# A DLRM tower on one core: the units split 114/81 in the first block and 82/113 in the later ones (from 110/85), the layer 1 matrix reloaded once, and a newly planned order

## The chip, the core and the metric

The kernel runs on one core of a Trainium2 chip, in float32. The metric is the device time of one execution in microseconds. The profile is one execution, recorded on that core; its page gives the span from the first to the last instruction, and this span is what the rows below are about.

## What is computed

```python
e = jnp.stack([tbl_0[ids[:, 0]], ..., tbl_39[ids[:, 39]]], axis=1)   # 2048 x 40 x 64
i_idx, j_idx = np.triu_indices(40, k=1)                             # 780 pairs
viW = jnp.einsum('bpd,pde->bpe', e[:, i_idx, :], W)                 # W: 780 x 64 x 64
z = jnp.einsum('bpe,bpe->bp', viW, e[:, j_idx, :])
h = jnp.concatenate([z, dense_ctx], axis=1)                         # 2048 x 796
h = jnp.maximum(h @ W_top1 + b_top1, 0.0)                           # 796 x 512
h = jnp.maximum(h @ W_top2 + b_top2, 0.0)                           # 512 x 256
y = h @ W_top3                                                      # 256 x 1
```

Each of 2048 examples looks up 40 rows of 64 numbers. For each of the 780 pairs of fields, one row goes through a 64x64 matrix and is multiplied with the other row and summed over 64. The 780 sums and 16 dense inputs go through three layers.

## The kernel before, in words

The batch is worked in four blocks of 512 examples. Two neighbouring fields form a duo, so there are 20 duos, and four duos form a quad, so there are 5 quads. A block has 190 pairings of two different duos (four field pairs each) and 20 pairs inside the duos. Its work on TensorE is cut into 195 **units**, and each unit ends in one product of 128x1024 numbers on VectorE (DVE).

- A standing unit (F, line 1007) holds weights still and streams the transposed rows `x`. Its result lies with the 64 numbers of a pair along the partitions, so VectorE writes the product to `fprod` (line 1172) and TensorE has to sum it with a matmul against `ones` into `z_ps` (line 1032). One unit has two such sum tiles; four tiles go side by side in one **round**, so two F units take one round.
- A moving unit (R, line 1003) holds `x` still and streams weights. Its result has the 64 numbers along the row, so no TensorE sum is needed. The product (line 1163, line 1158 for the inner units I) is summed over 64 by one of three engines: ScalarE (ACT, tile `rprod_A`, 16 activations with an accumulator each, line 1234), VectorE (`rprod_V`, one reduce, line 1180) or GpSimd (POOL, `rprod_P`, six additions, lines 919 and 926). The sums are gathered in `zb`, which TensorE turns later in pieces (event `zr`, line 1049).

`MOVED` says for each quad how many of the duos go by R units. Before, it is `[0, 3, 4, 5, 8]` for all blocks: 110 F units, 80 R units (four per pairing of a quad with a duo) and 5 I units in each block.

Around the units TensorE turns looked-up rows into `x` (event `duo`, line 965; the first four duos come from tables on chip instead, line 958), and runs the three layers of the block before (events `l1`, `l2`, `l3`; four `l1` of 7 passes each, line 1063, two `l2`, line 1073). The first-layer matrix `w1_sb` lies in `mlp_sb`, loaded once by SP at line 874. Its rows stand in the order in which the sums come out, so that order depends on the split of the units.

Three semaphore rings couple the engines. `u_ps` has `U_SLOTS` = 3 places: unit u waits until the product of unit u-3 is done. `fprod` has 9 places, freed by the TensorE sums. `rprod` has 3, 2 and 2 places for A, V and P, freed by the sum over 64. Weights come in by SP through `wf_ring` (4 places of two F units, line 829) and `wr_ring` (2 places of four R units, line 835).

The order on every engine is fixed when the program is built. The class `Plan` walks through the work with a small clock of its own: it has a duration for each kind of step, picks the next step for TensorE (unit, sum, duo or layer step), gives each R unit's sum to A, P or V, and places GpSimd's lookups (line 899) between its sums. Before, sums go in groups of `GROUP` = 4 F units, which are two rounds. Lookups of later blocks carry waits on `mains_done`, so that on average over six of them they start no closer than `T_PACE` = 1.6 us:

```python
if len(self.gather_at) >= PACE_OVER:
    gather_at = max(gather_at, self.gather_at[-PACE_OVER] + PACE_OVER * T_PACE)
```

In the first block, each lookup is followed by a memset of a spare piece (line 908) that keeps them apart.

Of the kernel before, what the change touches and what calls it, by code (L numbers as in the profile page):

```python
# [35 lines left out]
P = 128  # L36
# [10 lines left out]
MOVED = [0, 3, 4, 5, 8]  # L47
FOLD = 2 * 8
GROUP = 4
HALF = GROUP // 2  # L50
# [6 lines left out]
Z_SPARE = 2  # L57
# [20 lines left out]

STANDING = [("F", n, k) for n in range(DUOS) for k in range(MOVED[n // 4], n)]
CHUNKS_R = [(q, k) for q in range(QUADS) for k in range(MOVED[q])]  # L80
MOVING = [unit for q in range(QUADS) for unit in
          [("R", c, s) for c, (of, _) in enumerate(CHUNKS_R) if of == q for s in range(SUBS)] + [("I", q, 0)]]
NF, NR = len(STANDING), len(MOVING)
NC = len(CHUNKS_R)
GROUPS = -(-NF // GROUP)

HALVES = NF // HALF
NT = 2 * NF
Z_TILES = 64
K_GROUPS = Z_TILES // (2 * GROUP)  # L90
ZF = -(-NT // Z_TILES)
Z_LAST = NT - Z_TILES * (ZF - 1)
R_PAIRS = NC * FOLD + DUOS
ZR = -(-R_PAIRS // P)
ZK = ZF + ZR

ZB_SLOTS = ZR + 2
DENSE = 16

STRIPS = 4  # L100

DENSE_CHUNK, DENSE_ROW = ZK - 1, R_PAIRS % P
assert 0 < DENSE_ROW <= P - DENSE


def z_rows(k):

    if k == DENSE_CHUNK:
        return DENSE_ROW + DENSE
    return P if k < ZF else min(P, R_PAIRS - P * (k - ZF))  # L110


W1_COLS, W2_COLS = ZK * H1, M1 * H2
assert NF % HALF == 0 and Z_TILES % (2 * GROUP) == 0

# [11 lines left out]
def tile_pairs(f, half):  # L127

    _, n, k = STANDING[f]
    i, j = 2 * (DUOS - 1 - n) + half, 2 * (DUOS - 1 - k)  # L130
    return (i, j), (i, j + 1)


def moving_pair(c, half, e):

    q, k = CHUNKS_R[c]
    return 2 * (DUOS - 1 - 4 * q - e // 2) + e % 2, 2 * (DUOS - 1 - k) + half


# [4 lines left out]
def quad_of(kind, n):  # L144

    return n if kind == "I" else CHUNKS_R[n][0]


def stands(kind, n):

    return list(range(4 * n, 4 * n + 4)) if kind == "I" else [CHUNKS_R[n][1]]


def first_column(kind, n):

    return FOLD * NC + 4 * n if kind == "I" else FOLD * n


def units_until(c):

    return 1 + max(r for r, (kind, n, _) in enumerate(MOVING) if first_column(kind, n) < P * (c + 1))

def lay_standing(w):
    out = np.zeros((NF // HALF, P, HALF, P), np.float32)
    for f in range(NF):
        for half in range(2):  # L170
            for par, pair in enumerate(tile_pairs(f, half)):
                out[f // HALF, half * DIM:(half + 1) * DIM, f % HALF,
                    par * DIM:(par + 1) * DIM] = w[pair_index(*pair)]
    return out.reshape(NF // HALF, P, HALF * P)


def lay_moving(w):
    out = np.zeros((NC, P, 8, DIM), np.float32)
    for c in range(NC):
        for half in range(2):  # L180
            for e in range(8):
                out[c, half * DIM:(half + 1) * DIM, e] = w[pair_index(*moving_pair(c, half, e))].T
    return out.reshape(NC, P, 8 * DIM)
# [13 lines left out]
def lay_mlp(w1, b1, w2, b2, w3):  # L197
    lay1 = np.zeros((P, ZK, H1), np.float32)
    for t in range(NT):
        k, strip, r = z_place(t)  # L200
        for par, pair in enumerate(tile_pairs(t // 2, t % 2)):
            lay1[32 * strip + r + par, k] = w1[pair_index(*pair)]
    for c in range(NC):
        for a in range(FOLD):
            row = FOLD * c + a
            lay1[row % P, ZF + row // P] = w1[pair_index(*moving_pair(c, a // 8, a % 8))]
    for n in range(DUOS):
        row = first_column("I", n // 4) + n % 4
        lay1[row % P, ZF + row // P] = w1[pair_index(*inner_pair(n))]
    n_pairs = FIELDS * (FIELDS - 1) // 2  # L210
    lay1[DENSE_ROW:DENSE_ROW + DENSE, DENSE_CHUNK] = w1[n_pairs:]
    lay2 = w2.reshape(M1, P, H2).transpose(1, 0, 2)
    return np.concatenate([lay1.reshape(P, -1), lay2.reshape(P, -1), b1.reshape(M1, P).T, b2.reshape(M2, P).T,
                           w3.reshape(M2, P).T], axis=1)

T_UNIT, T_SUMS, T_DUO, T_PASS, T_TURN = 0.846, 0.41 * GROUP, 0.44, 0.858, 0.17
T_PROD, T_VSUM, T_PART, T_COPY, T_RELU = 1.131, 1.127, 0.48, 0.58, 0.69
# [5 lines left out]
T_INNER = 1.75  # L230
T_HOT, T_BUILD, T_TABLE, T_TABLES = 0.423, 0.535, 8.5, 1.6

LEAD, LEAST, ROWS_LEAD = 8, 1, 5

STALL, GAP = 0.05, -0.3

MLP_GAP, MLP_PACE = 8, 14

AHEAD, BEHIND = 2, 10
# [3 lines left out]
A_MOST, P_MOST = 1, 1  # L243


def tail_of(b):

    return [("l1", b, m) for m in range(M1)] + [("l2", b, m) for m in range(M2)] + [("l3", b, 0)]


class Plan:


    def __init__(self):
# [8 lines left out]
        self.queue = {e: [] for e in "VAP"}  # L263
        self.parts = []
        self.gathered, self.built = 2 * SUBS * HOT, 0
        self.gather_at, self.main_at, self.paced = [], [], 0
        self.need = 0
        self.f_units, self.r_units = [], []
        self.rows_of = {}
# [1051 lines left out]
```

## Time and profile before

| what | value |
|---|---|
| time, three runs | 1356.27 us median (1356.18 to 1361.23) |
| profiled execution, span | 1195.2 us |
| profiled execution, own time | not given apart from the span; median less span is 161.1 us, outside the first to last instruction |
| granted TensorE clock | 1.000 over the whole span |
| TensorE busy | 1177.7 us, 99% |
| VectorE busy | 1003.0 us, 84% |
| ScalarE busy | 966.7 us, 81% |
| GpSimd busy | 774.4 us, 65% |
| DMA | 79.7 MB, mean 67 GB/s |

Matmuls are recorded one by one though they overlap, so the busy share says that TensorE seldom stands still, and the chain of waits says what it does in that time. TensorE's first unit starts at 37.5 us; the first units of blocks 2, 3 and 4 start at 307.1, 592.0 and 875.4 us, and the last unit ends near 1155 us.

### The profile page before, as it was taken

What the parts mean: (1) busy time and instruction counts of PE and PEld (TensorE: products, weight loads), DVE (VectorE), ACT (ScalarE), POOL (GpSimd) and SP (SyncE); (2) the same over time, 40 slices, a digit from 0 to 9 for tenths busy, and PEclk for the clock granted to TensorE, in tenths of its full rate; (3) what the DMA queues carried; (4) which work ended last, traced back from release to release, by engine and by line L of the source; (5) the groups of instructions that cost most, each with busy time, mean ns of one, the idle gap of its engine ahead of it and who ended that gap; (6) DMA issues with size and microseconds to landing.
All of it is one profiled execution on the core that took longest, in us unless ns stands there. A gap on an engine that the chain in (4) does not pass through costs nothing.

```text
span 1195.2 us, 23954 instructions
## 1 busy us (share of the span) xinstructions
PE 1177.7 (99%) x6248; PEld 457.7 (38%) x6248; DVE 1003.0 (84%) x915; ACT 966.7 (81%) x7477; POOL 774.4 (65%) x1026
## 2 busy tenths in 40 slices
PE   7999999999999999999999999999999999999999
PEld 2433333333434343333434343433343434343333
DVE  7898999999588888999877878889978778888960
ACT  1295989899476799999687879999969899999971
POOL 8888883687656556677755557887765556634320
PEclk9999999999999999999999999999999999999999
DMA  7143232222222222222222222222222222211100
GB/s 211 38 148 78 65 75 65 70 72 72 57 56 68 56 67 73 68 67 70 71 55 63 60 64 65 71 63 78 73 57 59 59 66 63 66 45 55 49 10 0
DMA packets 68480, 79.73 MB, mean 67 GB/s; under 512 B 15308, under 2 KB 46028, under 8 KB 68216
## 3 DMA queue, kind: packets, MB, share of 16 engines
q1 hardware_dynamic: 48752, 58.10, 16.6%
q0 software_dynamic: 19456, 19.96, 9.3%
q8 instruction: 50, 0.82, 0.3%
q14 instruction: 86, 0.70, 0.2%
q10 hardware_dynamic: 136, 0.14, 0.1%
HBM read 78.14 MB, written 0.01 MB: 65 GB/s over the span
## 4 chain that ended last, share of the span: by engine, by line
PE 89%; DVE 5%; issue 4%; ACT 1%; POOL 1%; DMA 0%; SPq 0%; DVEq 0%; ACTq 0%; POOLq 0%
PE u_ps L1007 30%; PE u_ps L1003 23%; PE z_ps L1032 16%; PE turn_ps L1063 7%; PE turn_ps L965 3%; PE u_ps L997 3%; PE turn_ps L958 2%; DVE fprod L1172 2%; PE turn_ps L1073 2%; PE u_ps L1063 2%; DVE acts L1128 1%; DVE zb L1180 1%; DVE rprod_A L1163 1%; PE u_ps L1073 1%; ACT rprod_A L1234 1%
## 5 line engine op out<-in xcount | busy, mean ns | idle before, releaser
L1234 ACT ACTIVATE rprod_A<-rprod_A 128x64 f32<-128x64 f32 x3664 | 877.8, 243 | 95.2 <-DVE rprod_A L1163 66.5
L899 POOL DMA_INDIRECT rows<-in_tbl,ids_all x608 | 575.2, 946 | 288.6 <-issue 113.5
L1234 ACT ACTIVATION_READ_ACCUMULATOR rprod_A<-rprod_A 128x1 f32 x3664 | 691.6, 189 | 0.1
L1172 DVE TENSOR_TENSOR fprod<-u_ps,x 128x1024 f32<-128x1024 f32 x440 | 524.0, 1222 | 32.1 <-PE u_ps L1007 31.9
L1007 PE MATMUL u_ps<-x,wf_ring 64*128 64x512 f32 x1760 | 444.9, 604 | 2.3 <-DVE fprod L1172 0.7
L1163 DVE TENSOR_TENSOR rprod_A<-u_ps,rows 128x1024 f32<-128x1024 f32 x213 | 260.5, 1224 | 98.0 <-PE u_ps L1003 97.8
L1003 PE MATMUL u_ps<-wr_ring,x 64*128 64x512 f32 x1280 | 338.7, 614 | 0.1
L1007 PEld LDWEIGHTS u_ps<-x,wf_ring 64*128 64x128 f32 x1760 | 158.6, 186 | 219.4 <-issue 163.9
L1032 PE MATMUL z_ps<-fprod,ones 128*32 128x512 f32 x1760 | 212.4, 598 | 0.0
L919 POOL TENSOR_TENSOR rprod_P<-rprod_P 128x512 f32<-128x512 f32 (+4 forms) x235 | 142.5, 606 | 81.7 <-DVE rprod_P L1163 58.6
L1003 PEld LDWEIGHTS u_ps<-wr_ring,x 64*128 64x128 f32 x1280 | 110.2, 185 | 172.7 <-issue 92.8
L1032 PEld LDWEIGHTS z_ps<-fprod,ones 128*32 128x32 f32 x1760 | 45.9, 109 | 147.1 <-issue 73.2
L1217 ACT COPY x<-turn_ps 128x512 f32<-128x512 f32 x80 | 45.5, 569 | 55.1 <-PE turn_ps L958 29.9
L1063 PE MATMUL turn_ps<-acts,mlp_sb 128*128 128x512 f32 (+1 forms) x182 | 81.6, 599 | 0.9 <-ACT acts L1249 0.9
L1180 DVE TENSOR_REDUCE zb<-rprod_V 128x16 f32<-128x1024 f32 x64 | 77.5, 1225 | 1.2
L1163 DVE TENSOR_TENSOR rprod_V<-u_ps,rows 128x1024 f32<-128x1024 f32 x62 | 75.4, 1226 | 0.1
L1163 DVE TENSOR_TENSOR rprod_P<-u_ps,rows 128x1024 f32<-128x1024 f32 x45 | 55.0, 1223 | 2.7 <-PE u_ps L1003 2.7
L965 PEld LDWEIGHTS turn_ps<-ident,rows 128*128 128x128 f32 x304 | 31.8, 140 | 57.0 <-issue 55.4
L1063 PEld LDWEIGHTS turn_ps<-acts,mlp_sb 128*128 128x128 f32 (+1 forms) x182 | 33.5, 190 | 47.6 <-issue 46.5
L965 PE MATMUL turn_ps<-ident,rows 128*128 128x128 f32 x304 | 49.9, 286 | 0.0
L958 PE MATMUL turn_ps<-acts,mlp_sb 125*64 125x512 f32 x136 | 36.4, 622 | 9.8 <-DMA mlp_sb<-in_tbl 7.8
L908 POOL MEMSET zb<- 128x256 f32 x128 | 46.0, 360 | 0.1
(45 smaller groups left out, 299.4 us busy)
## 6 DMA issues: line engine op xcount, KB each, us to landing
wf_ring<-in_w_standing SPq DMA_DIRECT2D x220, 128.0 KB
wr_ring<-in_w_moving SPq DMA_DIRECT2D x80, 256.0 KB
rows<-in_tbl,ids_all POOLq DMA_INDIRECT x608, 2.5
mlp_sb<-in_mlp SPq DMA_DIRECT2D x1, 2308.0 KB
mlp_sb<-in_tbl SPq DMA_DIRECT2D x6, 224.0 KB
wi_ring<-in_w_inner SPq DMA_DIRECT2D x20, 64.0 KB, 1.8
rows<-in_first_ids SPq DMA_DIRECT2D x4, 256.0 KB, 6.2
rprod_P<-in_first_ids SPq DMA_DIRECT2D x4, 256.0 KB, 8.8
```

What stands on the lines that cost most here:

```text
L899: nc.gpsimd.indirect_dma_start(rows[:, v % ROW_SLOTS, s, par * DIM:(par + 1) * DIM], None, tables[f], bass.IndirectOffsetOnAxis(ap=ids_all ...
L919: nc.gpsimd.tensor_tensor(of[:, :, 0:width], of[:, :, 0:width], of[:, :, width:2 * width], ALU.add).then_inc(fold_step, 1)
L958: op = pe.matmul(bank[h % 2 * DIM:(h % 2 + 1) * DIM, :], tables_sb[:, at:at + DIM], hot[0:HOT_PARTS, i % HOT_SLOTS, :], start=(c == 0), st ...
L965: op = pe.transpose(bank[:, s * P:(s + 1) * P], rows[:, v % ROW_SLOTS, s, :], ident[:])
L1003: op = pe.matmul(u_ps[:, bank + half, :], x[on, x_slot(b, of[0]), k * P:(k + 1) * P], wr_ring[on, c % WR_SLOTS, :], start=True, stop=True)
L1007: op = pe.matmul(u_ps[:, bank + half, :], wf_ring[on, c % WF_SLOTS, f % HALF * P:(f % HALF + 1) * P], x[on, x_slot(b, n), :], start=True, ...
L1032: op = pe.matmul(z_ps[32 * strip:32 * strip + 32, :], ones[:, 30 - row:62 - row], fprod[:, f % FPROD_SLOTS, t % 2, :], start=(r < STRIPS), ...
L1063: op = pe.matmul(bank[:, :], w1_sb[0:n_rows, k, m * P:(m + 1) * P], z_sb[0:n_rows, z_slot(b, k), :], start=(k == 0), stop=(k == ZK - 1))
L1163: nc.vector.tensor_tensor(products_of(u).rearrange("p h (a d) -> p h a d", a=4), u_ps[:, bank:bank + 2, :].rearrange("p h (a d) -> p h a d ...
L1172: nc.vector.tensor_tensor(fprod[:, f % FPROD_SLOTS], u_ps[:, bank:bank + 2, :], other, ALU.mult).then_inc(prods_done, 1)
L1180: nc.vector.tensor_reduce(to, of.rearrange("p (a s) d -> p a s d", a=to.shape[1]), AX.X, ALU.add).then_inc(r_sums["V"], 1)
L1234: op = nc.scalar.activation(of[:, j, :], of[:, j, :], ACT.Copy, accum_out=sum_at(u, j))
```

## The change

Each block has its own shape: `MOVED` becomes a list of four splits. The first block has 114 F, 76 R and 5 I units, each later one 82 F, 108 R and 5 I. The first-layer matrix is laid out for both splits, and SP loads the second layout once, after the first block's last `l1`. Sums are taken by rounds (one to three at once) instead of by groups of two rounds. The planner has new durations and rules; `T_PACE` becomes 1.25, the duration it has for one lookup, for all blocks but the first. Inner sums, `zb` and the ring of `z` tiles get new places. The number of 128-row pieces that layer 1 reads stays at 7.

```diff
-MOVED = [0, 3, 4, 5, 8]
+MOVED = [(0, 4, 4, 4, 7), (0, 4, 4, 7, 12), (0, 4, 4, 7, 12), (0, 4, 4, 7, 12)]
...
-GROUP = 4
-HALF = GROUP // 2
+HALF = 2
...
-T_GATHER, T_ROWS, T_FOLD = 1.25, 2.5, 3.3
-T_PACE, PACE_OVER, AHEAD_OF = 1.6, 6, 1.0
+T_GATHER, T_ROWS, T_FOLD = 1.25, 2.5, 3.65
+T_PACE, T_PACE_FIRST, PACE_OVER, AHEAD_OF = 1.25, 1.6, 6, 1.0
...
-AHEAD, BEHIND = 2, 10
+AHEAD, BEHIND = 0, 4
...
-A_MOST, P_MOST = 1, 1
+SUM_LEAST, SUM_MOST, SUM_WAIT, FOLLOW = 1, 3, 0.2, 0
+CHAIN = 0
+A_MOST, P_MOST, V_MOST = 2, 2, 1
...
+    def sums_ready(self, at):
+        if self.next_half() is None:
+            return 0
+        b, h = self.next_half()
+        n, stop = 0, min(SHAPES[b].halves, (h // Z_HALVES + 1) * Z_HALVES)
+        while h + n < stop:
+            ready = self.half_ready(b, h + n)
+            if ready is None or ready > at:
+                break
+            n, at = n + 1, at + T_ROUND
+        return n
...
+W1_AFTER = {unit_after(("l1", b, M1 - 1)): b for b in range(NB - 1) if KIND_OF[b] != KIND_OF[b + 1]}
...
-                    sp.dma_start(mlp_sb[:], mlp_w).then_inc(mlp_in, 16)
+                    sp.dma_start(mlp_sb[:], mlp_w[KIND_OF[0]]).then_inc(mlp_in, 16)
+                if u in W1_AFTER:
+                    old = W1_AFTER[u]
+                    sp.wait_ge(turned, TURN_AT["l1", old, M1 - 1] + 1)
+                    sp.dma_start(mlp_sb[:, 0:W1_COLS], mlp_w[KIND_OF[old + 1]][:, 0:W1_COLS]).then_inc(mlp_in, 16)
```

Over the program, as counted in the two orders: F units 440 before and 360 now, R units 320 and 400, sum rounds 220 and 180, sum batches 112 and 126, `zr` turns 12 and 15, duos 80 and 80, layer steps the same. The sums over 64 of R and I units lie on ACT, V and P as 229, 64 and 47 before, and as 251, 103 and 66 now. By block, V has 25, 20, 13 and 6 before and 18, 33, 35 and 17 now; P has 7, 10, 13 and 17 before and 2, 16, 15 and 33 now; ACT has 53, 55, 59 and 62 before and 61, 64, 63 and 63 now.

TensorE's order in the second block, before; `z_ps<-fprod,ones` is a batch of sums (x8 is two rounds), `u_ps<-x,wf_ring` an F unit for each x2, `u_ps<-wr_ring,x` an R unit for each x2, `turn_ps<-ident,rows` a duo:

```order
L1003 MATMUL u_ps<-wr_ring,x 128x512 x2
L1007 MATMUL u_ps<-x,wf_ring 128x512 x2
L1003 MATMUL u_ps<-wr_ring,x 128x512 x2
L1007 MATMUL u_ps<-x,wf_ring 128x512 x2
L1032 MATMUL z_ps<-fprod,ones 32x512 x8
L1003 MATMUL u_ps<-wr_ring,x 128x512 x2
L1007 MATMUL u_ps<-x,wf_ring 128x512 x2
```

The same engine in the second block now; `turn_ps<-acts,mlp_sb` x7 is one `l1`:

```order
L1111 MATMUL z_ps<-fprod,ones 32x512 x4
L1085 MATMUL u_ps<-x,wf_ring 128x512 x2
L1081 MATMUL u_ps<-wr_ring,x 128x512 x2
L1111 MATMUL z_ps<-fprod,ones 32x512 x4
L1081 MATMUL u_ps<-wr_ring,x 128x512 x2
L1085 MATMUL u_ps<-x,wf_ring 128x512 x2
L1043 MATMUL turn_ps<-ident,rows 128x128 x4
L1081 MATMUL u_ps<-wr_ring,x 128x512 x2
L1143 MATMUL turn_ps<-acts,mlp_sb 128x512 x7
L1081 MATMUL u_ps<-wr_ring,x 128x512 x8
L1111 MATMUL z_ps<-fprod,ones 32x512 x4
```

A batch is often one round where it was always two (one at the end of a block), R units follow one another, and fewer F units stand between the batches.

GpSimd's order where the first block's lookups end, before; each `in_tbl` row is a run of lookups, each `rprod_P` row a step of one sum over 64:

```order
L908 MEMSET zb 128x256
L899 DMA rows<-in_tbl_38,ids_all 128x64 x4
L899 DMA rows<-in_tbl_39,ids_all 128x64 x4
L899 DMA rows<-in_tbl_36,ids_all 128x64 x4
L899 DMA rows<-in_tbl_37,ids_all 128x64 x2
L919 TENSOR_TENSOR rprod_P<-rprod_P 128x16x32
```

GpSimd at the same place now:

```order
L986 MEMSET zb 128x256
L977 DMA rows<-in_tbl_38,ids_all 128x64 x4
L977 DMA rows<-in_tbl_39,ids_all 128x64 x4
L977 DMA rows<-in_tbl_36,ids_all 128x64 x4
L977 DMA rows<-in_tbl_37,ids_all 128x64 x4
L977 DMA rows<-in_tbl_34,ids_all 128x64 x4
```

There were 14 lookups before the first sum over 64; now 64 stand in a row before it. Of the lookups and sums together, 344 lookups carried a wait on `mains_done` before, and 336 do now, in other places.

SP's order at the new load, now (`mlp_sb<-in_mlp` 128x3584 is the second layout of the first-layer matrix); before, the row is not there:

```order
L900 DMA wf_ring<-in_w_standing 128x256
L907 DMA wr_ring<-in_w_moving 128x512
L900 DMA wf_ring<-in_w_standing 128x256
L952 DMA mlp_sb<-in_mlp 128x3584
L907 DMA wr_ring<-in_w_moving 128x512
L913 DMA wi_ring<-in_w_inner 128x128
L900 DMA wf_ring<-in_w_standing 128x256 x2
```

One load of 1792 KB now stands ahead of the ring loads behind it.

## Rows read from the trace of the kernel before

**Rows 1.** The page: busy time, share of the span and instructions of each engine.
```profile
PE 1177.7 (99%) x6248; PEld 457.7 (38%) x6248; DVE 1003.0 (84%) x915; ACT 966.7 (81%) x7477; POOL 774.4 (65%) x1026
```

**Rows 2.** Windows: first block, second, third, fourth, tail; PE, PEld, DVE, ACT, POOL busy.
```profile
37.50:307.10 269.60, 266.89 (x1485) 99.96 (x1484) 257.45 (x235) 222.70 (x1729) 211.09 (x310) 1.00 0.30 77
307.10:592.00 284.90, 283.89 (x1533) 111.92 (x1534) 245.09 (x215) 231.99 (x1796) 189.13 (x226) 1.00 0.27 65
592.00:875.40 283.40, 282.51 (x1530) 111.44 (x1526) 239.92 (x210) 245.13 (x1921) 197.21 (x243) 1.00 0.27 66
875.40:1154.10 278.70, 278.32 (x1493) 107.58 (x1492) 228.09 (x200) 252.27 (x1998) 145.84 (x199) 1.00 0.22 55
1154.10:1195.20 41.10, 38.00 (x110) 15.23 (x108) 3.36 (x3) 7.57 (x24) 0.00 (x0) 1.00 0.00 0
```

**Rows 3.** The chain of waits in the second block: start, length, what.
```profile
400.28 1.85 PE z_ps L1032 x16
402.13 1.06 PE u_ps L1003 x4
403.19 1.72 PE u_ps L1007 x8
404.91 0.59 PE turn_ps L965 x4
405.50 1.06 PE u_ps L1003 x4
...
408.27 6.21 PE turn_ps L1063 x14
```

**Rows 4.** The chain of waits, shares by line: stretch 150 to 306 us.
```profile
by line: PE u_ps L1007 26.9%; PE u_ps L1003 24.7%; PE z_ps L1032 13.1%; issue 12.8%; DVE fprod L1172 6.9%; DVE rprod_A L1163 3.6%; DVE zb L1180 3.0%; PE turn_ps L965 2.6%; PE u_ps L997 2.5%; ACT rprod_A L1234 1.7%; DVE rprod_V L1163 1.6%; P
```

**Rows 5.** Windows: the stretch 150 to 306 us, columns as in rows 2.
```profile
150.00:306.00 156.00, 154.50 (x854) 56.45 (x850) 154.22 (x137) 142.37 (x1130) 110.44 (x155) 1.00 0.28 70
```

**Rows 6.** Timeline of VectorE around 200 us: start, length, instruction.
```profile
200.29 1.25 DVE L1163 TENSOR_TENSOR rprod_V<-u_ps,rows 128x1024 f32<-128x1024 f32 x1
201.42 1.25 DVE L1172 TENSOR_TENSOR fprod<-u_ps,x 128x1024 f32<-128x1024 f32 x1
```

**Rows 7.** The chain of waits at a turn of `zb`, end of the second block.
```profile
590.54 0.56 PE turn_ps L1049 x4
```

**Rows 8.** Timeline of VectorE behind one `l1` of the second block; idle before in brackets.
```profile
329.18 2.36 DVE L1163 TENSOR_TENSOR rprod_A<-u_ps,rows 128x1024 f32<-128x1024 f32 x2 [7.90 <-PE u_ps L1003]
```

**Rows 9.** Groups by line: busy time, mean ns of one, idle before and its releasers.
```profile
L1234 ACT ACTIVATE rprod_A<-rprod_A 128x64 f32<-128x64 f32 x3664 | 877.8, 243 | 95.2 <-DVE rprod_A L1163 66.5 <-DVE rprod_A L1158 26.2 <-ACT acts L1269 1.3
```

**Rows 10.** Instructions that touch `mlp_sb`: the one load of the layer matrices.
```profile
L874 SPq DMA_DIRECT2D mlp_sb<-in_mlp x1: 432/432/432, 62.8 to 62.8; - x1
```

**Rows 11.** Windows: the 5 us behind that load, columns as in rows 2.
```profile
65.00:70.00 5.00, 5.00 (x28) 2.15 (x24) 4.60 (x5) 4.40 (x35) 4.39 (x8) 1.00 0.94 396
```

**Rows 12.** Timeline of GpSimd: first and last of six lookups in a row.
```profile
661.10 0.94 POOL L899 DMA_INDIRECT rows<-in_tbl,ids_all  x1 [0.30 <-issue]
...
667.35 0.94 POOL L899 DMA_INDIRECT rows<-in_tbl,ids_all  x1 [0.30 <-issue]
```

**Rows 13.** Timeline of GpSimd: one sum over 64 (without its last step), next lookup.
```profile
791.64 3.37 POOL L919 TENSOR_TENSOR rprod_P<-rprod_P 128x512 f32<-128x512 f32 x5
...
795.52 0.96 POOL L899 DMA_INDIRECT rows<-in_tbl,ids_all  x1 [0.22 <-issue]
```

**Rows 14.** Timeline of GpSimd in the first block: two lookups, a memset between.
```profile
62.84 0.95 POOL L899 DMA_INDIRECT rows<-in_tbl,ids_all  x1 [0.17 <-issue]
...
64.28 0.95 POOL L899 DMA_INDIRECT rows<-in_tbl,ids_all  x1 [0.16 <-issue]
```

**Rows 15.** Instructions of the lookups' line: min/median/max ns of all 608.
```profile
L899 POOL DMA_INDIRECT rows<-in_tbl,ids_all x608: 938/944/1097, 3.9 to 1035.0; - x152
```

**Rows 16.** The chain of waits around an inner unit, end of the second block.
```profile
583.61 1.96 PE u_ps L997 x32
...
589.41 1.13 PE u_ps L1007 x4
```

More of the change, by code:

```diff
@@ new lines, with starts @@
+KINDS = sorted(set(MOVED))
+SHAPES = [Shape(moved) for moved in MOVED]
+KIND_OF = [KINDS.index(moved) for moved in MOVED]
+ZK, ZR = max(shape.zk for shape in SHAPES), max(shape.zr for shape in SHAPES)
+Z_RING = 9 - ZR
+ZB_SLOTS = 5
+def starts(counts):
+    return [sum(counts[:b]) for b in range(NB + 1)]
+F_FROM, R_FROM = starts([shape.nf for shape in SHAPES]), starts([shape.nr for shape in SHAPES])
+HALF_FROM, Z_FROM = starts([shape.halves for shape in SHAPES]), starts([shape.zf for shape in SHAPES])
@@ L177, in lay_moving @@
-def lay_moving(w):
[L178 to L183, printed above, removed]
+def lay_standing(w):
+    out = []
+    for shape in map(Shape, KINDS):
+        part = np.zeros((shape.halves, P, HALF, P), np.float32)
+        for f in range(shape.nf):
+            for half in range(2):
+                for par, pair in enumerate(shape.tile_pairs(f, half)):
+                    part[f // HALF, half * DIM:(half + 1) * DIM, f % HALF,
+                         par * DIM:(par + 1) * DIM] = w[pair_index(*pair)]
+        out.append(part.reshape(shape.halves, P, HALF * P))
+    return np.concatenate(out)
@@ L186, in lay_inner @@
+def lay_moving(w):
+    out = []
+    for shape in map(Shape, KINDS):
+        part = np.zeros((shape.nc, P, 8, DIM), np.float32)
+        for c in range(shape.nc):
+            for half in range(2):
+                for e in range(8):
+                    part[c, half * DIM:(half + 1) * DIM, e] = w[pair_index(*shape.moving_pair(c, half, e))].T
+        out.append(part.reshape(shape.nc, P, 8 * DIM))
+    return np.concatenate(out)
 def lay_inner(w):
@@ L484, in do_back, with next_half, half_ready @@
         self.arrived[n] = self.bank_at = self.do_act(("copy", ("back", 0, n)), self.pe_t + LAG_PE, T_COPY)
-    def do_sums(self, b, g):
-        self.order.append(("sum", b, g))
-        first = NF * b + GROUP * g
+    def next_half(self):
+        h = len(self.half_at)
+        if h >= HALF_FROM[NB]:
+            return None
+        b = max(a for a in range(NB) if HALF_FROM[a] <= h)
+        return b, h - HALF_FROM[b]
+    def half_ready(self, b, h):
+        f = F_FROM[b] + HALF * h + HALF - 1
+        if f >= len(self.f_units):
+            return None
+        at = self.prod_at[self.f_units[f]]
+        return max(at, self.z_at[-1]) if h % Z_HALVES == 0 and self.z_at else at
@@ L596, in run @@
[L596 to L601 removed]
+                step_at = self.step_ready(steps[0]) if steps and turned > self.need + LEAST else None
+                soon = self.pe_t + max(stall, SOON)
@@ L1087, in _ @@
             pe.wait_ge(ones_done, 1)
-            for what, b, n in ORDER:
+            for what, b, n, *more in ORDER:
                 if what == "duo":
@@ L1095, in _ @@
                 elif what == "sum":
-                    sums(b, n)
+                    sums(b, n, more[0])
                 elif what == "zr":
```

482 lines of the change are left out of this document (254 added, 228 removed).

## The prediction

> **What bounds the kernel now.** I read the page first. TensorE is busy for 99% of the span, VectorE for 84%, ScalarE for 81%, GpSimd for 65% [rows 1]. A busy TensorE can still be a waiting one, since its records overlap, so the next view is the chain of waits. In the second block the chain is TensorE alone, one piece against the next [rows 3]: a unit takes 0.86 us, two rounds of sums 1.85, a duo 0.59, an `l1` 6.21, and the first unit behind anything that isn't a unit takes 1.06 in place of 0.86. (The trace records two instructions for each one that the order shows.) A wait there would show as a piece of another engine, and there is none.
>
> The first block is different. In the stretch 150 to 306 us the chain passes through VectorE's lines again and again, with 12.8% issue between [rows 4], and VectorE is busy 154.22 of 156 us [rows 5]. So the first block runs at VectorE's pace and the other three at TensorE's. The windows by block say the same: VectorE has 257 of 270 us in the first, 245 of 285 in the second, 240 of 283 in the third, 228 of 279 in the fourth [rows 2].
>
> **Prices.** Taken from start to start, one VectorE product or reduce is 1.13 us (200.29 to 201.42) [rows 6]. A round costs 0.86, since a batch of two rounds takes 1.85, of which 0.13 is entry. With the 0.20 that the next unit pays, each batch costs 0.33 beside its rounds [rows 3]. A duo costs 0.59 and the same 0.20, 0.79 in all; a turn of `zb` 0.56 and 0.20, 0.76 in all [rows 3, 7]. An F and an R unit cost TensorE and VectorE the same, so swapping 80 of them moves only sums.
>
> **Blocks 2 to 4, on TensorE.**
> - Each has 28 F units fewer, so 14 rounds fewer (41 for 55): 14 x 0.86 = 12.0 us, three times, -36.0.
> - Batches in this stretch grow from 86 to 87, +0.3. Although most batches are now one round, there are fewer rounds to batch.
> - Turns of `zb` grow from 9 to 14: 5 x 0.76 = +3.8.
> - Duos that stand in these blocks grow from 54 to 57 (the planner does four more in the second and one fewer in the last): 3 x 0.79 = +2.4.
> - Layer 1 keeps its 7 pieces, so the `l1` pieces of 6.21 us don't change.
>
> That is -29.5 us. By block it is -7.3 in the second, -11.2 in the third and -11.0 in the fourth.
>
> **What hides the added sums, and what it costs if the cover is thin.** VectorE gets 195 products and 33, 35 and 17 sums in the later blocks: 228, 230 and 212 instructions at 1.13, which is 258, 260 and 240 us. Without new waits the blocks would last 278, 272 and, less the tail, 268 us. So VectorE would be busy 93%, 96% and 90%, where it was at 86%, 85% and 82%. It can't use all its time: while an `l1` holds TensorE, it gets no product, and stood idle 7.90 us across one [rows 8]. Today it comes to such a step with nothing in hand. With three products in `u_ps` and two sums in `rprod_V` waiting, five instructions or 5.7 us, the hole would shrink to 2.2 us. Four `l1` then cost some 9 us a block, two `l2` little. 260 and 9 is 269, just under 272. TensorE and VectorE would be level, and level engines with a three-place ring between them lose something to each other. The lower bound is nothing. The upper is what the first block loses with VectorE saturated: 269.6 us against 220 instructions, 249 us, hence 21 us, part of which is its start. I take 2 us in each of blocks 2 and 3, near the lower end because the third block's row is still on TensorE's side: +4.
>
> ScalarE gets 251 sums for 229. A sum's 16 activations took 877.8/229 = 3.8 us busy by overlapping records [rows 9], so each later block has 63 or 64 of them, about 242 us of 270, with the copies beside them. That is up from 55 to 62. It is tight also, but a copy late by one pair of activations (0.5 us) only matters when TensorE waits for that bank; it is within the 4 us.
>
> **The first block, on VectorE.** Its V sums go from 25 to 18: 7 x 1.13 = -7.9 us where VectorE sets the pace. TensorE gets two rounds (+1.7) and 13 batches (+4.3) more there, 3 duos and 2 `zb` turns fewer (-3.9), which is +2.1; these lie in its waiting. I take -7, between -8 (all hidden) and +2 (no stall removed at all).
>
> **The reload.** SP issues 1792 KB ahead of the ring loads. The load before was 2308 KB, issued at 62.8 [rows 10]; in 65 to 70 us the DMA engines were 0.94 busy at 396 GB/s, and TensorE was busy 5.00 of 5.00 us [rows 11]. At that rate the reload takes 4.6 us. `wr_ring` holds four more R units then, at least 3.4 us of units and, with F units between, twice that. So I cost it at 0. Uncovered, it is up to 5 us, once. Nothing else waits on SP's queue but the rings, and the matrix is first read one block later.
>
> **Lookups and GpSimd.** A lookup back to back takes 1.25 us from start to start (six in a row start within 6.25 us) [rows 12], and a sum over 64 takes 3.88 until the next lookup starts [rows 13]; in the first block a lookup with its memset is 1.44 [rows 14]. At present: 47 x 3.88 + 128 x 1.44 + 480 x 1.25 = 967 us. After: 66 x 3.88 in place of 47, 1040 us, against some 1120 until the last unit ends. It still fits, with 80 us to spare, so the pacing's removal and 19 more sums cost nothing, and earlier rows remove no wait either, as the chain shows none for rows [rows 3]. The 608 lookups last 938 to 1097 ns with a median of 944 [rows 15], next to a VectorE that is nearly always at work. If more VectorE work held them back, the maximum would be far from the median already. The Trainium skill, SBUF — State Buffer, "SBUF: two separate sides", says that VectorE in a two-port mode locks GpSimd out, so that it can't write the descriptors of its transfers. [...] The trace agrees with the case in which no lock is taken.
>
> **The sum.** -29.5 + 4 - 7 = -32.5 us. The span goes from 1195.2 to 1162.7. I keep the 161.1 us around it (the median less this span; the median of three stands for the profiled one, whose own time isn't given), and get 1323.8. One more thing is in the order's favour: in the later blocks the chain still leaves TensorE now and then, as for 3.8 us behind an inner unit at 583.6 [rows 16], though TensorE has other units for a part of that. The new order is planned with durations nearer to the rows (0.858 us for a unit in place of 0.846), and may avoid some of it; I choose -2, which no row fixes. Forecast: 1322 us, 2.5% faster.
>
> **Rivals.**
> - VectorE becomes the bound in blocks 2 and 3 as it is in the first. For it: 93 and 96% by the above. Against: `l1` holes shrink when work is in hand. If these blocks lost to each other what the first loses beyond its start, about 10 us each in place of 2, the time is 1322 + 16 = 1338. From 97% of a block's length on it decides.
> - The order's gains are larger: the first block, planned with 7 fewer V sums and batches of one round, drops its waits nearly to TensorE's own work, some 12 us more. Then 1310.
> - Slower: lookups in long runs. The rows show six in a row at 1.25 [rows 12]; in the new order 64 stand in a row, with waits among them. If a lookup in a long run took what the planner spaced them at before, 1.6 us, 480 x 0.35 = 168 us would be added to GpSimd, 88 more than its spare time; rows come late, duos wait, and the time is 1322 + 88 = 1410. It decides from 1.25 + (80 + 34 + 7)/480 = 1.50 us for a lookup on. Against it: the six show no creep, the last like the first (0.94 long, 0.30 between) [rows 12].
> - It doesn't do what it says: GpSimd or ring waits return the rounds' 34 us to other waits, as a change of order can. Then 1350 to 1356. The three engines at 90 to 96% each speak for it, the pure TensorE chain of the later blocks against.
>
> **Chances.** Forecast (1314 to 1330) 0.58; VectorE bound (1330 to 1345) 0.17; larger gain (below 1314) 0.15; given back (within 0.5% of 1356) 0.06; slower by lookups 0.04. A measurement tells about 0.5%, 7 us, from no change. Faster holds the first three and a bit, 0.91; same 0.05; slower 0.04. The range 1308 to 1338 takes in the larger gain's 1310 and the bound's 1338, and leaves out about 2 in 10.
>
> **What the profile after would show.** 1440 records of TensorE's sums for 1760. Blocks 2 to 4 start-to-start near 278, 274 and 270 us, the first near 263. VectorE busy around 90% of the span. The chain in the third block still mostly TensorE, with more pieces of VectorE than now. Lookups' median 944 ns, and 1.25 us between starts in the run of 64. TensorE unbroken in the 10 us behind the new load. I'm wrong if lookups in the run are above 1.5 us apart, if a block after the first is longer than 280 us, or if the first block hasn't become shorter.

## The result, and the profile after

The changed kernel takes 1387.7 us (median of four runs, 1383.15 to 1392.04) against 1356.22 us before. The ratio is 1.0229, 95% interval 1.0199 to 1.0259: slower by 2.3%, where 2.5% faster was forecast.

The page after, its first two parts (busy time by engine, and the 40 slices with the granted clock), in answer to [rows 1]:

```profile
span 1386.4 us, 24251 instructions
PE 1220.5 (88%) x5940; PEld 460.6 (33%) x5940; DVE 1057.5 (76%) x954; ACT 1076.0 (78%) x8181; POOL 834.0 (60%) x1140
PE   7864878998889888888998998888998989899999
POOL 8888282036555665666585666666656665566860
PEclk9966978999998999999999999999999999999999
```

The first line overturns a premise. This execution took 1388.46 us and its span is 1386.4: there are 2 us around the span, not 161. If the same holds for the kernel before, its timed runs of 1356 us have no span of 1195, and the one profile that was shown of it is of an execution with less waiting. The first experiment settles that. TensorE is busy for 88% and not 99%, and its clock falls in the first block.

The windows by block (columns as in [rows 2]), first the changed kernel:

```profile
37.20:405.10 367.90, 295.08 (x1497) 106.33 (x1496) 252.68 (x226) 252.07 (x1919) 204.49 (x291) 0.88 0.21 57
405.10:729.30 324.20, 291.15 (x1423) 112.17 (x1424) 264.13 (x229) 276.59 (x2104) 202.66 (x257) 0.97 0.24 63
729.30:1052.30 323.00, 292.46 (x1446) 110.77 (x1442) 264.88 (x231) 271.90 (x2079) 200.00 (x251) 0.97 0.22 58
1052.30:1341.90 289.60, 273.27 (x1372) 103.24 (x1368) 244.09 (x213) 258.44 (x2038) 193.59 (x289) 0.99 0.20 52
```

The first block has 98 us more than [rows 2], the second and third 39 and 40, the fourth 11. In the second block TensorE is busy 90% and ScalarE 85%, so neither explains its length. The chain of waits names the piece but not the reason. From 405 to 1340 us it is:

```profile
by line: ACT rprod_A L1315 36.0%; PE u_ps L1081 18.3%; PE u_ps L1085 14.8%; issue 9.2%; PE z_ps L1111 6.8%; PE turn_ps L1143 2.7%; PE turn_ps L1043 1.9%; PE u_ps L1075 1.9%; ACT x L1298 1.2%; DVE rprod_A L1243 1.2%; PE turn_ps L1153 1.2%; D
...
562.51 3.81 ACT rprod_A L1315 x32
```

More than a third is ScalarE's sums over 64, at their usual length: one sum of 32 records takes 3.81 us. TensorE's own pieces have their old lengths too (an `l1` of 14 records takes 6.21 us at 1201.43, as in [rows 3]). The reason is in the timeline of the first block, with GpSimd and ScalarE side by side (start, length, instruction, idle before it and until what):

```profile
83.13 0.95 POOL L977 DMA_INDIRECT rows<-in_tbl,ids_all  x1 [0.17 <-issue]
83.51 0.20 ACT L1315 ACTIVATION_READ_ACCUMULATOR rprod_A<-rprod_A 128x1 f32 x1 [0.85 <-issue]
...
84.57 0.95 POOL L977 DMA_INDIRECT rows<-in_tbl,ids_all  x1 [0.17 <-issue]
84.97 0.26 ACT L1315 ACTIVATE rprod_A<-rprod_A 128x64 f32<-128x64 f32 x1 [0.78 <-issue]
...
86.01 0.95 POOL L977 DMA_INDIRECT rows<-in_tbl,ids_all  x1 [0.17 <-issue]
86.44 0.26 ACT L1315 ACTIVATE rprod_A<-rprod_A 128x64 f32<-128x64 f32 x1 [0.51 <-issue]
...
87.46 0.95 POOL L977 DMA_INDIRECT rows<-in_tbl,ids_all  x1 [0.17 <-issue]
87.88 0.26 ACT L1315 ACTIVATE rprod_A<-rprod_A 128x64 f32<-128x64 f32 x1 [0.85 <-issue]
```

Four times, 0.38 to 0.43 us after a lookup starts, ScalarE comes out of a gap of 0.5 to 0.85 us that ends on issue: nothing that the profile shows was missing. The first of the four lies between an activation and the read of its accumulator. There is no semaphore between these two, so a gap there can't be a wait that the program asked for. I call such gaps **holds**. They can be summed over a whole trace (the last column is the idle time before these reads); first the kernel before as in the rows, then the changed one:

```profile
L1234 ACT ACTIVATION_READ_ACCUMULATOR rprod_A<-rprod_A 128x1 f32 x3664 | 691.6, 189 | 0.1
L1315 ACT ACTIVATION_READ_ACCUMULATOR rprod_A<-rprod_A 128x1 f32 x4016 | 768.5, 191 | 61.4 <-issue 60.9
```

TensorE has much longer gaps. Here are two of its pieces, and VectorE's product between them:

```profile
111.05 2.13 PE L1085 MATMUL u_ps<-x,wf_ring 64*128 64x512 f32 x4 [0.69 <-issue]
127.00 1.23 DVE L1252 TENSOR_TENSOR fprod<-u_ps,x 128x1024 f32<-128x1024 f32 x1 [14.97 <-remote]
128.28 2.08 PE L1081 MATMUL u_ps<-wr_ring,x 64*128 64x512 f32 x4 [15.10 <-issue]
```

The page says "issue" for TensorE's gap of 15.10 us, but it is a wait: the unit needs the product of the unit three before it (ring `u_ps`). Counted in order, that is the product shown, which ends at 128.23, 0.05 us before TensorE goes on. VectorE in turn waits for `mains_done`, the signal that TensorE gives at the end of a unit. The last pass of the unit in question is recorded until 107.37 us, and VectorE is let go only at 127.00, at the same time as SP's next load, which waits for `mains_done` too. The ends of matmuls are modelled, so the trace doesn't tell whether the passes stood still or their signal was late. I call both a **late finish**. In the changed kernel's first block 26 products start more than 3 us after the last recorded pass of their unit, 222 us in all; in the first block of [rows 2] there is one, 5.4 us.

Windows of the same stretch and of one in which GpSimd sends nothing:

```profile
110.00:120.00 10.00, 2.49 (x5) 0.58 (x4) 2.03 (x2) 4.69 (x32) 8.84 (x15) 0.53 0.12 25
120.00:130.00 10.00, 1.72 (x4) 0.50 (x4) 1.34 (x2) 1.59 (x11) 8.84 (x15) 0.50 0.16 36
150.00:160.00 10.00, 9.32 (x50) 3.35 (x50) 9.71 (x9) 8.40 (x68) 0.00 (x0) 1.00 0.13 43
160.00:170.00 10.00, 10.00 (x76) 4.28 (x72) 10.00 (x10) 10.00 (x85) 0.00 (x0) 1.00 0.22 68
```

With GpSimd busy 8.84 of 10 us, TensorE has 2.49 and 1.72 us of work, VectorE 2.03 and 1.34, ScalarE 4.69 and 1.59; with GpSimd at 0.00, all three are busy for 84% or more. In the whole trace the lookups themselves are as before, in answer to [rows 15]:

```profile
L977 POOL DMA_INDIRECT rows<-in_tbl,ids_all x608: 938/944/1097, 4.0 to 1196.1; - x152
```

So nothing on GpSimd looks slower. It is the others that stand.

### The profile page after: what moved, and what is told of

Its sections match the earlier page's. It is cut to its first block, busy times and chain, and to the rows that moved or that the text cites. A ratio compares the mean times of both kernels' runs of the same rounds, so it can differ in the third digit from the quotient of the medians.

```text
span 1386.4 us, 24251 instructions
## 1 busy us (share of the span) xinstructions
PE 1220.5 (88%) x5940; PEld 460.6 (33%) x5940; DVE 1057.5 (76%) x954; ACT 1076.0 (78%) x8181; POOL 834.0 (60%) x1140
## 4 chain that ended last, share of the span: by engine, by line
PE 58%; ACT 26%; issue 11%; DVE 4%; another core or an unknown queue 1%; DMA 0%; SPq 0%; DVEq 0%; ACTq 0%
ACT rprod_A L1315 24%; PE u_ps L1085 18%; PE u_ps L1081 18%; PE z_ps L1111 9%; PE turn_ps L1036 3%; PE turn_ps L1143 2%; PE turn_ps L1043 2%; PE u_ps L1075 2%; DVE fprod L1252 1%; DVE rprod_A L1243 1%; PE u_ps L1143 1%; ACT x L1298 1%; PE turn_ps L1153 1%; PE turn_ps L1129 1%
## 5 line engine op out<-in xcount | busy, mean ns | idle before, releaser
L1315 ACT ACTIVATE rprod_A<-rprod_A 128x64 f32<-128x64 f32 x4016 | 963.5, 245 | 93.8 <-issue 68.1
L1315 ACT ACTIVATION_READ_ACCUMULATOR rprod_A<-rprod_A 128x1 f32 x4016 | 768.5, 191 | 61.4 <-issue 60.9
L1252 DVE TENSOR_TENSOR fprod<-u_ps,x 128x1024 f32<-128x1024 f32 x360 | 431.2, 1218 | 116.5 <-remote 57.3
L1081 PE MATMUL u_ps<-wr_ring,x 64*128 64x512 f32 x1600 | 427.8, 630 | 62.0 <-issue 27.5
L1085 PE MATMUL u_ps<-x,wf_ring 64*128 64x512 f32 x1440 | 396.5, 636 | 53.5 <-issue 18.3
L997 POOL TENSOR_TENSOR rprod_P<-rprod_P 128x512 f32<-128x512 f32 (+4 forms) x330 | 200.0, 606 | 83.8 <-DVE rprod_P L1243 63.0
L1243 DVE TENSOR_TENSOR rprod_V<-u_ps,rows 128x1024 f32<-128x1024 f32 x101 | 122.4, 1219 | 20.5 <-remote 7.6
L1260 DVE TENSOR_REDUCE zb<-rprod_V 128x16 f32<-128x1024 f32 x103 | 122.9, 1211 | 0.5
L1075 PE MATMUL u_ps<-wi_ring,x 64*128 64x64 f32 x640 | 43.2, 279 | 4.3 <-issue 3.1
L1075 PEld LDWEIGHTS u_ps<-wi_ring,x 64*128 64x128 f32 x640 | 41.1, 195 | 16.2 <-issue 16.1
```

Source lines behind the costliest of these rows:

```text
L997: nc.gpsimd.tensor_tensor(of[:, :, 0:width], of[:, :, 0:width], of[:, :, width:2 * width], ALU.add).then_inc(fold_step, 1)
L1075: op = pe.matmul(u_ps[:, bank + half, to], x[on, x_slot(b, of[2 * half + a]), s * P:(s + 1) * P], wi_ring[on, I_AT[u] % WI_SLOTS, a * DIM: ...
L1081: op = pe.matmul(u_ps[:, bank + half, :], x[on, x_slot(b, of[0]), k * P:(k + 1) * P], wr_ring[on, c % WR_SLOTS, :], start=True, stop=True)
L1085: op = pe.matmul(u_ps[:, bank + half, :], wf_ring[on, c % WF_SLOTS, f % HALF * P:(f % HALF + 1) * P], x[on, x_slot(b, n), :], start=True, ...
L1243: nc.vector.tensor_tensor(products_of(u).rearrange("p h (a d) -> p h a d", a=4), u_ps[:, bank:bank + 2, :].rearrange("p h (a d) -> p h a d ...
L1252: nc.vector.tensor_tensor(fprod[:, f % FPROD_SLOTS], u_ps[:, bank:bank + 2, :], other, ALU.mult).then_inc(prods_done, 1)
```

## Experiments

Two theories stand against each other through most of them. A: lookups hold up the other engines, the more the closer they come. C: level engines cost the time, by the split's added sums over 64. All ratios are to the kernel before on the same chip. That kernel took 1356 to 1363 us on most chips and 1329 on the chip of three of the runs, so times of different chips are compared by ratio. What makes the chips differ isn't known, so a ratio across them is good to about 2%. The lengths of blocks come from one execution each, and the first block can differ by 20 us: three kernels with the same order in it show 368, 351 and 347.5 us.

**The kernel before once more, unchanged (one run).**

> The kernel before, unchanged, to see where its 1356 us lie: the profile of the changed kernel has a span only 2 us below its time, while the one profile of before had 161 us between them. Theory A (waits inside the span): this profile's span is about 1354 us, and the 160 us that the earlier profile lacked are stretches in which TensorE, ScalarE and VectorE sit on issue while GpSimd sends lookups, most of them in the first block. Rival B (fixed cost outside the span): the span is again 1195 us.

1352.93 us, span 1351.0. Its windows by block, then its row of ScalarE's waits on issue (us in total, times, longest), then that row of the changed kernel:

```profile
38.10:398.60 360.50, 288.87 (x1485) 106.18 (x1484) 261.30 (x234) 230.05 (x1729) 211.31 (x311) 0.91 0.21 58
398.60:714.60 316.00, 299.10 (x1533) 114.87 (x1534) 246.95 (x214) 237.46 (x1796) 189.72 (x227) 0.97 0.22 59
714.60:1018.80 304.20, 289.61 (x1532) 109.91 (x1528) 240.16 (x209) 249.53 (x1921) 197.07 (x242) 1.00 0.23 61
1018.80:1310.00 291.20, 283.10 (x1495) 107.92 (x1494) 228.41 (x200) 254.61 (x1998) 146.20 (x198) 0.99 0.19 52
```

```profile
ACT rprod_A L1234 <- issue: 96.2, 153, 9.1
```

```profile
ACT rprod_A L1315 <- issue: 129.0, 263, 8.1
```

Among the waits of the earlier profile of this very program there is no such row. Late finishes are back as well: 36 products of the first block start more than 3 us late. So B falls: 156 us that the earlier profile lacked are inside the span, 91 of them in the first block. The changed kernel's loss against this trace is 7 us in the first block, 8 and 19 in the second and third, 4 in the tail, and a gain of 2 in the fourth.

**The pace, on the changed kernel.** (In this kernel and those built on it, the planner also looks further ahead on GpSimd where it has no unit at hand, 8 us for 2. With the pace at 1.25 that gives the very order of the changed kernel, so it is the pace that makes the difference.)

```diff
-T_PACE, T_PACE_FIRST, PACE_OVER, AHEAD_OF = 1.25, 1.6, 6, 1.0
+T_PACE, T_PACE_FIRST, PACE_OVER, AHEAD_OF = 1.6, 1.6, 6, 1.0
```

> The changed kernel with the lookups of the later blocks planned 1.6 us apart over six again. Theory A (lookups hold up the other engines' issue, and closer lookups more): the later blocks lose less to issue, ratio to before 0.97 to 1.00. Rival C (the three engines level at 90 to 96% are what costs, the lookups' pace is not): 1.02 to 1.04, since rows come later.

1360.02 us, ratio 1.0021 (1.0001 to 1.0040), 2% below the changed kernel. ScalarE's wait on issue falls from 129.0 to 80.5 us. That is just above what A expected and below C's range. The pace is a mean over six lookups, and the distance from one lookup to the next hardly changes: in blocks 2 to 4, 264 of them start less than 1.3 us after the one before, for 299 in the changed kernel. The order of the sums moves too (247 on ScalarE for 251), so the run shows what the pace is worth, and not that the distance is what counts.

**The old split under the new planner.**

```diff
-MOVED = [(0, 4, 4, 4, 7), (0, 4, 4, 7, 12), (0, 4, 4, 7, 12), (0, 4, 4, 7, 12)]
+MOVED = [(0, 3, 4, 5, 8)] * 4
```

> The changed kernel with the old split 110/85 in all blocks, so that no matrix is reloaded; planner, order rules and lookups' pace are the new ones. Theory A (pace and order cost, the split gains): slower than the changed kernel or equal, ratio to before 1.02 to 1.06. Rival C (the split's added sums over 64 cost): 0.98 to 1.00.

1417.56 us, ratio 1.047 (1.0432 to 1.0509). Against the changed kernel's 1.0229 that is 2.4%, some 30 us, slower. So the new split gains what its fewer rounds promised, and everything else in the change costs about 60 us. C, as the cause of the loss, falls. Under the new rules the old split has 254 sums on ScalarE and 47 on VectorE, for 229 and 64 in the kernel before, so the rules load ScalarE even without the new split.

**The pace alone, on the kernel before** (the first block keeps its 1.6).

```diff
-T_PACE, PACE_OVER, AHEAD_OF = 1.6, 6, 1.0
+T_PACE, T_PACE_FIRST, PACE_OVER, AHEAD_OF = 1.27, 1.6, 6, 1.0
...
-                self.pool_t = gather_at + (T_PACE if v < DUOS else T_GATHER)
+                self.pool_t = gather_at + (T_PACE_FIRST if v < DUOS else T_GATHER)
```

> The kernel before with one number changed: its lookups in the later blocks are planned 1.27 us apart over six in place of 1.6 (at 1.25 its planner finds no order). Split and rules are the old ones. Theory A (close lookups hold up the other engines' issue): ratio to before 1.01 to 1.03, the whole of it in the later blocks. Rival C (only a kernel whose engines are level by the new split suffers): 0.995 to 1.005.

1407.84 us, ratio 1.0359 (1.0318 to 1.0401). One number makes the old kernel slower than the change did. The order moves with it: the planner gives GpSimd 61 sums where it gave 47, and VectorE 46 for 64. ScalarE's holds can't be the reason: its idle time before accumulator reads is 32.1 us here as in the repeat of the kernel before, and its wait on issue is 95.8 us for 96.2. What the closer lookups do to this kernel is open. The expectation was too small, and its "whole of it in the later blocks" was wrong: the first block rose too, from 361 to 377 us.

**The pace, and one waiting sum in place of two on ScalarE and on GpSimd.**

```diff
-A_MOST, P_MOST, V_MOST = 2, 2, 1
+A_MOST, P_MOST, V_MOST = 1, 1, 1
```

> The changed kernel with the lookups planned 1.6 us apart again and with the old limit of one waiting sum on ScalarE and on GpSimd (two in the changed kernel), so that ScalarE gets fewer sums (221 for 247 in the run with the pace alone). Theory A with its second part (holds delay a ScalarE without slack, and TensorE then waits for it): faster than before, ratio 0.98 to 0.99. Rival D (ScalarE's load doesn't matter, VectorE's does, which gets 142 sums for 110): slower than the pace alone, 1.01 or more.

1342.51 us, ratio 0.9884 (0.9841 to 0.9927), against 1.0021 with the pace alone. ScalarE has 221 sums for 247, GpSimd 57 for 63, and VectorE 32 more. D falls: it is worth time to take sums off ScalarE. That a ScalarE with fewer sums has room to catch up after a hold fits, but no run shows it by itself.

**No lookups in blocks 2 to 4** (one run; memsets of the same rows; later blocks compute on constants).

```diff
+                if v >= DUOS:
+                    nc.gpsimd.memset(rows[:, v % ROW_SLOTS, s, par * DIM:(par + 1) * DIM],
+                                     0.5).then_inc(fills, 1)
+                    return
                 nc.gpsimd.indirect_dma_start(
```

> The changed kernel with the lookups of blocks 2 to 4 replaced by a memset of the same rows by GpSimd, at the same places of its order and behind the same waits; the first block's lookups stay. The later blocks compute on constants. Theory A: the later blocks last what the prediction had, 270 to 280 us each (324, 323 and 290 to the last unit in the changed kernel), and the first block stays near 368. Rival C (level engines, no matter what GpSimd sends): the later blocks stay above 305 us.

1245.38 us. The blocks last 351, 273, 275 and 263 us; rival C wanted more than 305 for the later ones. With the lookups gone, the split, the order and the three level engines give what the prediction had.

**Plain loads in blocks 2 to 4** (one run; the same queue and bytes, rows that follow one another, so the wrong ones).

```diff
+                if v >= DUOS:
+                    nc.gpsimd.dma_start(rows[:, v % ROW_SLOTS, s, par * DIM:(par + 1) * DIM],
+                                        tables[f][P * s:P * (s + 1), :]).then_inc(rows_in[v % ROW_SLOTS], 16)
+                    return
```

> The changed kernel with the lookups of blocks 2 to 4 replaced by plain loads from GpSimd's queue: the same 128x64 destination, from 128 rows of the table that lie one after another, at the same places and behind the same waits. The later blocks compute on the wrong rows. Theory J (what holds the other engines is the indirect form, in which GpSimd reads 128 indices and works out 128 addresses): the later blocks fall to 270 to 285 us as with the memsets. Theory K (any transfer whose descriptors GpSimd writes holds them): they stay near 320 us.

1242.24 us. Its windows by block, GpSimd's plain loads (min/median/max ns), and the reads of ScalarE's accumulators in the whole trace:

```profile
38.70:386.20 347.50, 289.53 (x1497) 105.22 (x1496) 251.52 (x225) 249.74 (x1919) 177.21 (x289) 0.89 0.22 61
386.20:659.70 273.50, 273.36 (x1422) 109.17 (x1422) 260.87 (x229) 269.36 (x2104) 137.46 (x257) 1.00 0.26 74
659.70:934.30 274.60, 274.51 (x1446) 108.12 (x1442) 262.48 (x231) 263.19 (x2080) 134.80 (x253) 1.00 0.24 68
934.30:1197.40 263.10, 263.10 (x1374) 103.63 (x1370) 242.56 (x213) 254.40 (x2038) 154.41 (x287) 1.00 0.20 58
```

```profile
L978 POOL DMA_DIRECT2D rows<-in_tbl x480: 534/537/578, 294.7 to 1051.3; - x160
```

```profile
L1319 ACT ACTIVATION_READ_ACCUMULATOR rprod_A<-rprod_A 128x1 f32 x4016 | 764.0, 190 | 11.8 <-issue 11.4
```

TensorE is busy 273.36 of 273.50 us, VectorE 95% and ScalarE 98% of the block, and nothing is lost. In blocks 2 to 4 alone ScalarE's idle time before accumulator reads is 0.0 us here and 44.8 in the changed kernel, with the same order on every engine. K falls: a transfer that GpSimd sets up costs the others nothing in itself. What holds them comes with the indirect lookups. Three things changed at once, though: GpSimd reads no indices, it is busy for 537 ns and not 944, and the rows that the transfer fetches lie one after another. The run doesn't tell these apart.

**A longer memset behind the first block's lookups.**

```diff
-        pause = zb[:, ZB_SLOTS - 1, 0:2, :].rearrange("p s c -> p (s c)")
+        pause = zb[:, ZB_SLOTS - 1, 0:4, :].rearrange("p s c -> p (s c)")
```

> The changed kernel with the memset behind each lookup of the first block twice as long (512 columns for 256), so that these lookups start about 1.7 us apart and not 1.44. Theory A: fewer holds; the first block lasts 20 to 60 us less than 368, or, where rows then come late, the holds per lookup fall all the same. Rival E (a lookup holds the others for its own time, whatever the distance): the first block is as long or longer.

1315.95 us, ratio 0.9690 (0.9635 to 0.9745). The first block:

```profile
41.70:331.70 290.00, 271.07 (x1497) 101.67 (x1496) 251.90 (x227) 244.43 (x1919) 228.36 (x292) 0.98 0.28 73
```

78 us come off it, with lookups 1.65 us apart and not 1.44; the other blocks stay as they were (324, 324, 289). In this first block 6 products start more than 3 us late, where there were 26. A gap of 0.2 us more between 128 lookups outweighs all of the change. E falls.

**The same on the kernel before.**

> The kernel before with the longer memset behind the first block's lookups alone. Theory A: its first block goes from 361 to some 290 us too, ratio 0.94 to 0.96. Rival G (only the order of the changed kernel profits): 0.98 to 1.00.

1275.26 us, ratio 0.9575 (0.9537 to 0.9612); first block 288 us. Late finishes there go from 36 to 4. So the longest piece of waiting was in both kernels, and the change had no part in it.

**Pace, ScalarE's load and the long memset together.**

> The version with the pace 1.6 and one waiting sum on ScalarE (0.988 of before), with the longer memset behind the first block's lookups on top (which took the changed kernel from 368 to 290 us there). Theory A: the two lie in different blocks and add up, ratio to before 0.92 to 0.95. Rival F (the longer memset only moves the lookups' holds into the second block): 0.96 to 0.98.

1262.70 us, ratio 0.9504 (0.9479 to 0.9529), just above A's range and below F's. Had the two ratios multiplied, it would be 0.936. By blocks they do add up: the first lasts 279.5 us here for 355 without the long memset, 76 less, where the memset alone brought 78. The ratio falls short since this chip took 1329 us for the kernel before and the other 1361.

**A memset behind every later lookup too.**

```diff
+                if v >= DUOS:
+                    spaces.append(v)
+                    if len(spaces) > 1:
+                        pool.wait_ge(spaced, len(spaces) - 1)
+                    nc.gpsimd.memset(space[:], 0.0).then_inc(spaced, 1)
...
-T_GATHER, T_ROWS, T_FOLD = 1.25, 2.5, 3.65
+T_GATHER, T_ROWS, T_FOLD = 1.45, 2.5, 3.65
```

> As the version with pace, one waiting sum and long memset, and in the later blocks each lookup is followed by a memset of 256 columns as well (about 1.44 us from lookup to lookup, planned as 1.45), so that no two lookups there start 1.25 us apart. Theory A in its sharper form (it is the distance from one lookup to the next that counts, not the mean over six): later blocks shorter by 5 to 20 us each, ratio 0.90 to 0.93. Rival H (the mean pace counts, and the memsets only fill GpSimd): equal to the version without them or slower, since rows come later.

1248.89 us, ratio 0.9386 (0.9366 to 0.9406). Better than without, but short of the range: the second and third blocks last 308 and 297 us, for 310 and 298 in the run without. So the expected 5 to 20 us a block didn't come there; the first and the fourth are 5 and 6 us shorter. ScalarE's idle time before accumulator reads is 0.1 us in the whole trace, with all 608 indirect lookups in it, so these blocks of 308 and 297 us have another cause than its holds. The order moved as well (VectorE 148 sums for 142).

**The same with rows earlier** (`T_PACE` 1.45, and `A_MOST, P_MOST, V_MOST = 2, 1, 1`).

> The changed kernel with its split, the long memset behind the first block's lookups, a memset of 256 columns behind each later lookup, lookups planned 1.45 us apart with no further pacing, and one waiting sum on GpSimd (two stay allowed on ScalarE). In the run before this one with memsets everywhere the holds were gone from the later blocks, and what was left of them were planned waits for rows that came late by the pace of 1.6. Theory A: with rows earlier, blocks 2 and 3 last 285 to 298 us, ratio to before 0.91 to 0.94. Rival I (holds come back when ScalarE has 252 sums again): 0.95 or more.

1265.64 us, ratio 0.9317 (0.9277 to 0.9357), the best ratio of all: 6.8% below the kernel before. (In microseconds the run before this one is the shortest, on the faster chip.) Its second and third blocks last 306 and 300 us, above the 285 to 298 that I expected. Rival I, 0.95 or more, falls.

**That order without the later memsets.**

> The run above with the memsets of the later blocks left out and nothing else changed: the same order on every engine and the same waits, but two lookups can start 1.25 us apart. Theory A in its sharper form (the distance from one lookup to the next counts): holds on ScalarE return, and the time is 1 to 4% above the run above. Rival H (only the mean pace counts): equal within 0.5%.

1273.93 us (1273.59 to 1278.53), against 1264.52 to 1268.42 with them on the same chip: 0.7% slower. That is less than A's 1 to 4% and more than the 0.5% that H allowed, and the runs don't overlap. ScalarE's idle time before accumulator reads is 21.4 us here and 12.2 with the memsets. So with the same order the distance from one lookup to the next (1.25 or 1.44 us) counts a little in the later blocks, where in the first block (1.44 or 1.65) it counts for much. That is little for the sharper form of A.

## Why the prediction was wrong, point by point

- **The 161.1 us around the span** were the first failed step. I took the median less the span as a fixed cost outside it, and built the sum on a trace of an execution that the timed runs don't resemble. The repeat of the kernel before had 2 us outside and 156 us more inside, most of it in the first block. A gap of 12% between a profile's span and the time stood in the table, and I gave it half a sentence.
- **"The pacing's removal and 19 more sums cost nothing"** was the second, and it decided the sign. I asked whether GpSimd has time for the lookups (it has) and whether the lookups get slower (they don't, 944 ns as before), but not whether the other engines do. They do: the changed kernel's blocks 2 to 4 last 324, 323 and 290 us with lookups and 273, 275 and 263 without. The pace alone is worth 2.0% on the changed kernel and cost 3.6% on the old one. The rival "slower" had lookups in long runs as its place, but with a lookup of 1.5 us as its condition, and that never came: back to back they still start 1.25 us apart. So it had the sign right by another mechanism. Two of the signs that I had named for being wrong came true: later blocks above 280 us, and a first block that isn't shorter.
- **Blocks 2 to 4 on TensorE, -29.5 us** were right in kind and near in size. The split was worth some 30 us under the new planner, and with the indirect lookups away the three blocks last 273.5, 274.6 and 263.1 us where 278, 272 and 268 were forecast without new waits. That is 35.8 us below [rows 2], 6 more than forecast.
- **VectorE as a rival bound** didn't come true: it is 95% busy there with nothing lost. The 4 us for level engines were not needed. The engine without slack was ScalarE, 98%, and I had called it tight and costed it within those 4 us. That is borne out as long as nothing holds it; in the changed kernel more than a third of the later chain is its sums (1.8% in the kernel before), and one waiting sum less on it and on GpSimd is worth 1.4%.
- **The first block, -7 us**, isn't borne out. As it stands it is 7 us longer than in the repeat of the kernel before, and its waits are mostly late finishes. With the long memset, which takes most of them away, it lasts 290 us in the changed kernel and 288 in the old one. As one execution of each is known, a gain of a few us could be hidden.
- **The reload at nothing** is borne out where nothing else disturbs: in the run with plain loads, the second block, which has it, has TensorE busy for all but 0.14 us.
- **The Trainium skill's rule** named the wrong party. The Trainium skill, SBUF — State Buffer, "SBUF: two separate sides", says that VectorE can lock GpSimd out. No row shows that, the lookups keep 938 to 1097 ns. The same section says that ScalarE and TensorE never wait on anyone there; whatever the path is, ScalarE was held and TensorE's units finished late while lookups ran.

What adds up to the result, by the ratios and on 1356 us: -33 us by the split, +28 by the pace, and some 36 more by the rest of the planner's rules, +31 in all. Of the 36, the second waiting sum on ScalarE and GpSimd accounts for about 19; the last 17 are not traced to a rule. The pieces come from different orders, so they are sizes, not a ledger.

Open is what a lookup takes from the other engines. It is not just any transfer in GpSimd's queue, by the plain loads. It may be the reading of indices, the way in which the addresses are handed over, or the scattered rows that are fetched, and no run here tells these apart. Nor is it a matter of distance alone: the two orders with a memset behind every later lookup both have them 1.44 us apart or more, and ScalarE's idle time before accumulator reads is 0.1 us in one and 12.2 in the other. Why one profile of the kernel before shows no holds at all, and why its time differs by 2% from chip to chip, is also open.

## What to carry to other kernels

Compare a profile's span with the time of the timed runs before building on it; if they differ by much more than the 2 us of the runs here, the trace is of another execution, and the first thing to do is to take it again. A wait that the profile puts down to "issue" can be a wait for a signal that comes late: follow the ring by hand and see what ended just before. Where the chain says "issue" on several engines at once, look at what the remaining engine does at that moment. And try more room between indirect lookups: here 0.2 us more between 128 of them was worth 78 us in the first block, more than twice what 40 rounds less brought, while in the later blocks 0.2 us more brought 0.7%.

## What the runs showed of the hardware

- While GpSimd runs indirect lookups, ScalarE can be held, by 0.5 to 0.85 us again and again, also between an activation and the read of its accumulator: 61.4 us in the changed kernel's trace. TensorE's units can finish late, up to 19.6 us after their last recorded pass. Neither happens in every execution: the first trace of the kernel before has 0.1 us before accumulator reads, and the repeat of the same program 32.1.
- At 1.44 us from lookup to lookup, the changed kernel's first block lasted 368 us; at 1.65 us it lasted 290.
- A plain load by GpSimd takes 537 ns there for the lookup's 944. With 480 of them in blocks 2 to 4, ScalarE's idle time before accumulator reads is 0.0 us there.
- A TensorE that waits also loses its clock: in the stretch 120 to 130 us the granted clock is 0.50, its lower level of 1.2 GHz, after 10 us in which it was busy for 2.49, and the unit at 128.28 takes 2.08 us. In 160 to 170 us, after 10 us at 9.32 busy, it is at 1.00, the upper level of 2.4 GHz, where two units at 165.53 take 1.88 together.
